# Ternary layers of a six-part transformer kernel: the first unit of each half multiplies part by part, and VectorE casts the second feature tile

## The reference

```
x = x + attention(layernorm(x))          # 16 heads
x = x + ternary_ffn(layernorm(x))        # called f0 here
x = x + gated_delta(layernorm(x))
x = x + ternary_ffn(layernorm(x))        # f1, same weights
x = x + attention(layernorm(x))          # 16 heads
x = x + routed_ffn(layernorm(x))
x = x + latent_attention(layernorm(x))
x = x + routed_ffn(layernorm(x))
```

```
scale = mean(|W|) + 1e-8
Wq    = clip(round(W / scale), -1, 1) * scale      # for W_up, W_gate (1024x256), W_down (256x1024)
up    = x @ Wq_up.T                                # 1024 x 1024
gate  = x @ Wq_gate.T
out   = (silu(up) * gate) @ Wq_down.T              # 1024 x 256
```

## Time and profile before

| what | us |
|---|---|
| median of three runs | 1550.88 |
| the three runs | 1550.71, 1550.88, 1554.65 |
| profiled execution, device time | 1545.75 |
| its span, first to last instruction | 1544.0 |
| TensorE matmuls busy | 1339.6 (87%) |
| VectorE busy | 919.0 (60%) |
| ScalarE busy | 681.9 (44%) |
| GpSimd busy | 305.8 (20%) |
| mean granted TensorE clock | 0.913 of full speed |

### The profile page before, as it was taken

The page is one execution under the profiler, slowest core; times in us unless marked ns, Lnnn a source line. Parts: engine busy times, 40 slices in busy tenths (PEclk is TensorE's granted clock), DMA queues, the critical chain, the costliest instruction groups (busy, mean ns, idle before and its releaser), DMA issues. The chain is left out here.

```text
span 1544.0 us, 31244 instructions
## 1 busy us (share of the span) xinstructions
PE 1339.6 (87%) x12873; PEld 752.5 (49%) x12881; DVE 919.0 (60%) x2164; ACT 681.9 (44%) x987; POOL 305.8 (20%) x394
## 2 busy tenths in 40 slices
PE   7999997987150998899999989999789999989999
PEld 3355544553130877363555545436235555555436
DVE  3899965744886246665999935433445555535431
ACT  5578786634250223644777762111334444442110
POOL 4340440001308000006100000110333434210110
PEclk9999998998665599998999998999679999998999
DMA  3222200000312100003222030000300000000000
GB/s 89 59 42 62 61 2 32 1 12 0 103 41 51 28 5 1 14 1 64 38 37 40 13 100 0 1 9 0 62 10 16 14 16 14 9 1 1 0 0 28
DMA packets 51808, 41.64 MB, mean 27 GB/s; under 512 B 26498, under 2 KB 41971, under 8 KB 51667
## 3 DMA queue, kind: packets, MB, share of 16 engines
q1 hardware_dynamic: 51666, 39.65, 11.9%
HBM read 20.33 MB, written 3.43 MB: 15 GB/s over the span
## 5 line engine op out<-in xcount | busy, mean ns | idle before, releaser
L586 DVE TENSOR_REDUCE row_max_pieces<-psum 128x1 f32<-128x512 f32 (+3 forms) x672 | 407.2, 647 | 125.0 <-PE psum L481 122.6
L685 ACT ACTIVATE probs<-psum 128x1024 f32<-128x1024 f32 (+7 forms) x384 | 343.8, 900 | 219.8 <-PE psum L481 219.4
L535 PE MATMUL psum<-probs,v_ones 128*32 128x256 f32 (+1 forms) x2688 | 239.3, 377 | 8.6 <-POOL probs L470 4.2
L481 PE MATMUL psum<-q_all,k_head 97*32 97x512 f32 (+3 forms) x1536 | 193.8, 497 | 3.5 <-issue 3.5
L481 PE MATMUL psum<-k_stack,q_stack 96*32 96x512 bf16 x2048 | 162.6, 387 | 5.5 <-DVE row_max_pieces L586 3.3
L481 PE MATMUL psum<-q_stack,k_stack 97*32 97x512 bf16 x2048 | 160.8, 385 | 0.0
L535 PEld LDWEIGHTS psum<-probs,v_ones 128*32 128x32 f32 x2688 | 88.6, 109 | 85.1 <-POOL probs L470 21.2
L481 PE MATMUL psum<-k_head_bf,q_all_bf 80*32 80x512 bf16 (+3 forms) x768 | 96.6, 349 | 5.2 <-POOL q_all_bf L2314 3.7
L481 PEld LDWEIGHTS psum<-q_all,k_head 97*32 97x32 f32 x1536 | 79.2, 110 | 34.9 <-issue 9.3
L481 PEld LDWEIGHTS psum<-k_stack,q_stack 96*32 96x32 bf16 x2048 | 58.2, 97 | 71.9 <-DVE row_max_pieces L586 20.4
L481 PEld LDWEIGHTS psum<-q_stack,k_stack 97*32 97x32 bf16 x2048 | 59.5, 97 | 50.7 <-issue 3.8
(11 more groups left out here) (324 smaller groups left out, 2096.0 us busy)
## 6 DMA issues: line engine op xcount, KB each, us to landing
q_stack<-arena SPq DMA_DIRECT2D x32, 96.0 KB, 2.7
k_stack<-arena SPq DMA_DIRECT2D x32, 96.0 KB, 2.7
arena<-gd_g_sums SPq DMA_DIRECT2D x6, 512.0 KB, 5.9
q_stack<-arena SPq DMA_DIRECT2D x32, 64.0 KB, 2.3
k_stack<-arena SPq DMA_DIRECT2D x32, 64.0 KB, 2.3
x_tokens<-in_x SPq DMA_DIRECT2D x4, 256.0 KB, 4.2
k_stack<-arena SPq DMA_DIRECT2D x32, 32.0 KB, 2.3
q_stack<-arena SPq DMA_DIRECT2D x32, 32.0 KB, 2.0
```

What stands on the lines that cost most here:

```text
L481: last = pe.matmul(o[j:j + 32], by[:, j:j + 32], rows, **flags)
L535: last = pe.matmul(psum[32 * g:32 * g + VW, PVB, a - g * D:D], V[:, c, h, :], pr[:, n % PB, a:(g + 1) * D], start=(c == 0), stop=(c == (2 ...
L586: last = dve.reduce_max(mx[:, h % 2, qt, i:i + 1], o[:, 0:plain], AX.X)
L685: act.activation(pr[:, n % PB, q_from(c):], psum[:, 2 * (n % 2):2 * (n % 2) + 2, :].rearrange("p a n -> p (a n)")[:, q_from(c):], ACT.Exp, ...
```

## The change

The semaphore `x_high_last` is new. In every half, ScalarE casts only k = 0 of the high part; VectorE casts k = 1 with a `tensor_copy` ahead of its first subtraction. TensorE no longer waits ahead of the first unit of a half for all low parts. In this unit it waits for the two high casts and multiplies the high part with up and with gate, then waits for the middle parts and does the same, then for the low parts. The other seven units of a half keep the order of before. Number and shape of the matmuls are unchanged, and so are the semaphores that they raise.

```diff
+    x_high_last = sem("_x_high_of_last_features")
...
-                    if e == 0:
-                        pe.wait_ge(x_low, KT * (half + 1))
                     if u >= 2:
                         pe.wait_ge(hid, u - 1)
-                    for j, w in enumerate((ups, gates)):
-                        for part in range(3):
-                            for k in range(KT):
-                                last = pe.matmul(psum[:, 2 * b + j, :], w[:, k, e * P:(e + 1) * P],
-                                                 XP[:, part, k, cols(half)],
-                                                 start=(part == 0 and k == 0), stop=(part == 2 and k == KT - 1))
-                        last.then_inc(proj, 1)
+
+                    def product(j, part):
+                        w = (ups, gates)[j]
+                        for k in range(KT):
+                            last = pe.matmul(psum[:, 2 * b + j, :], w[:, k, e * P:(e + 1) * P],
+                                             XP[:, part, k, cols(half)],
+                                             start=(part == 0 and k == 0), stop=(part == 2 and k == KT - 1))
+                        if part == 2:
+                            last.then_inc(proj, 1)
+
+                    if e == 0:
+                        pe.wait_ge(x_high, half + 1)
+                        pe.wait_ge(x_high_last, half + 1)
+                        for j in range(2):
+                            product(j, 0)
+                        pe.wait_ge(x_mid, KT * (half + 1))
+                        for j in range(2):
+                            product(j, 1)
+                        pe.wait_ge(x_low, KT * (half + 1))
+                        for j in range(2):
+                            product(j, 2)
+                    else:
+                        for j in range(2):
+                            for part in range(3):
+                                product(j, part)
...
-                    for k in range(KT):
-                        act.activation(XP[:, 0, k, cols(half)], XNT[:, k, cols(half)], ACT.Copy).then_inc(x_high, 1)
+                    act.activation(XP[:, 0, 0, cols(half)], XNT[:, 0, cols(half)], ACT.Copy).then_inc(x_high, 1)
...
+                    dve.tensor_copy(XP[:, 0, 1, cols(half)], XNT[:, 1, cols(half)]).then_inc(x_high_last, 1)
                     for k in range(KT):
-                        dve.wait_ge(x_high, half * KT + k + 1)
+                        dve.wait_ge((x_high, x_high_last)[k], half + 1)
                         dve.tensor_tensor(xr[:, k, cols(half)], XNT[:, k, cols(half)], XP[:, 0, k, cols(half)],
                                           ALU.subtract).then_inc(x_rest, 1)
```

## The result

Three comparisons of the two kernels were made, each on one chip. The first, with eight executions of each, is the result of record. In the third, one execution of the changed kernel was in a slow state (1572.63 us) and is left out.

What follows compares the result with a forecast made beforehand. TensorE, busy 87% of 1544.0 us, was taken as the bound. Gains of 1.59 and 2.10 us in the two ternary layers, 3.7 us together, taken from the median 1550.88 gave 1547.2 us; range 1542.8 to 1552.3.

Steps and rivals of the forecast that it cites:

- the two terms: Gains at unit 2 of the two ternary layers: 1.59 us in the first, 2.10 us in the second.
- the slow stretch at its longest: Outer case of slow-clock matmuls in both ternary layers: gains 1.59 and 1.37 us, 3.0 us in all.
- Step 2: Unit 0, between high, middle and low parts: the two new waits cost nothing at the slow clock.
- Step 3: End of units 0 and 1: 7 slow matmuls in the first ternary layer, unit 1 done at 261.46; 9 in the second.
- the sum's own outer case: First ternary layer, unit 0 with all 12 matmuls slow: units 0 and 1 done at 262.51.
- Step 4: Unit 2 waits for VectorE's first product: at 262.52 against 264.11 in the first ternary layer, 630.12 against 632.22 in the second.
- the chances 0.18, 0.13 and 0.03: Chances of a faster result: 0.18 from the forecast's own scatter, 0.13 for Rival A, 0.03 for B.
- the sum's passage to the end: Behind the ternary layers: their gains pass on to the next layers and the end, 3.7 us off the median.
- Rival A: Layers behind the first ternary one: the clock rises earlier there, 1 to 2 us more gain, about 1545.7 us; chance 0.13.
- B: Both ternary layers: the whole 2.74 us come through in each, 5.5 us, 1545.4 us; chance 0.03.
- C: Stall before unit 2 lowers the clock: 2.5 us lost per slow unit, 1552.3 us with one per layer; chance 0.06.
- D: End of the ternary layer: something there hides the gain, 1550.9 us; chance 0.08.

Runs made afterwards that it cites:

- cast_half0: Changed kernel, but VectorE casts k = 1 only in half 0 and ScalarE casts both tiles in half 1; ratio 0.9972 [0.9956, 0.9988] to the kernel before.
- after_delay_f0: Changed kernel with three idle ScalarE copies at the end of the first ternary layer; ratio 0.9967 [0.9951, 0.9983] to the kernel before.
- delay3_f1: Kernel before, with three idle ScalarE copies behind the last step of the second ternary layer; ratio 0.9995 [0.9980, 1.0010].
- delay6_f1: Kernel before, with six idle ScalarE copies behind the last step of the second ternary layer; ratio 1.0027 [1.0012, 1.0042].
- f0_only: Kernel before, with both parts of the change in the first ternary layer alone; ratio 0.9993 [0.9982, 1.0005].

## Why the prediction was wrong

**What held.** That VectorE's cast takes about 0.40 us and costs half 0 nothing: 0.43, and nothing. That TensorE starts 2.7 us sooner: 0.69 instead of 3.40 behind the first cast. That the SiLU slips by 0.32: 0.34. That the first product is late next in f1 and takes back part of the gain: it was, unit 2 at 630.19 against a forecast of 630.12, and cast_half0, which moves that product by 0.33 us, moved unit 2 by 0.33. The sizes of the two terms: 1.59 and 2.10 forecast, 1.6 and 2.0 in the first trace. In the other two traces of the changed kernel f1 gave 1.4, near the 1.37 that the sum had for the slow stretch at its longest.

**What failed inside the layers, without moving the sum.** Step 2 had TensorE run on into the middle parts, with k0's part needed first and k1's second. The code waits for both at once, and the trace has TensorE waiting to 256.77. Step 3 took seven slow matmuls over from before; the rise to full clock came at the same time as before, so the earlier start made them twelve, the sum's own outer case (262.51 without the stall). Step 4 had f0 bound by the product at 262.52. All twelve matmuls of unit 0 ran slow there, and with the stall in front of the middle parts TensorE itself came to 262.83; the product was at hand at 262.52. The 0.33 us at the end of f0 made up for it: the forecast's 1.59 was met by luck, with 1.23 from the steps that it named. A slip besides: the chances 0.18, 0.13 and 0.03 for a faster result add up to 0.34, not 0.32.

**The step that failed: the sum's passage to the end**, "The shift of 1.59 passes to the down products, the norm and the next layer" and "I apply the gain to the median". The sum counted the ternary layers alone and took every other layer at its old length. In the traces they did not keep it: the delta layer took 1.5 us back, the second attention layer added 2.0, and latent and last layer 1.8 in the mean: -1.6 + 1.5 - 2.0 - 2.0 - 1.8 = -5.9 us, with f1's term at its largest; with 1.4 for f1 it is -5.3, and the first routed layer adds -0.6. The three comparisons gave 3.9, 6.8 and 8.8, about 6.

How well is each term shown? The delta term is shown by one trace that only shifts the work (after_delay_f0), with its granted clock of 0.65 against 0.50, and by the group means, though three traces of 297 to 300 stand across both groups. Half of the attention term is shown: the sixteen matmuls differ by 1.0 us and follow the granted clock in the pair delay3_f1 and delay6_f1; the layer's whole 2.0 rests on group means that don't overlap. But these two terms nearly cancel (-0.5). What the measured gain has over the forecast, 2.3 us of about 6 and 5.1 of the 8.8 of record, must come mostly from the last terms and from the draw of executions, and for these there is no proof: the latent term rests on which of two kinds of latent layer a trace happened to show, and both kernels have both. So the step that failed is known, and where the surplus came from is open.

Rival A named the mechanism, in the delta layer and with 1 to 2 us more gain. There the sign was the other one (delta lost), and the rival had 0.13.

**The base.** 1550.88 was the median of three executions, and in the comparison of record it was right (1550.53): there the whole miss is in the gain. Later medians of the old kernel were 1546.6, 1549.1, 1548.1 and 1546.8, each of 31 or 35 executions, while the eight of the comparison of record gave 1550.5. The 8.8 us of that comparison are more than the traces can account for, and its interval and that of the second comparison don't meet (it ends at 0.9959, the other begins at 0.9961). Whether that is the chip or the draw of sixteen executions is open. With the medians of the second and third comparison, 1543.89 and 1542.9, the forecast's range would have held, which says how near the call was, not that it was right: a range of 9.5 us was drawn around a single sum while the old kernel's own executions spread over 8 to 10 us in every comparison (1543.66 to 1553.89 in the last).

**The other rivals.** B (all of 2.74 us in both layers) was rightly small: the SiLU stood where it had to. C (a stall that brings the grant down) didn't come: unit 2 of f1 behind the stall ran at the fast clock. D was half true of f0, by another way: f0_only's gain could not be measured, and the delta layer is where the traces have it given back. Rival A took the 7 and 9 slow matmuls of step 3 as a case of variation from run to run; they are two layers of one execution, and show no such variation by themselves. The drain that the Trainium skill adds to a table load (ScalarE: Activation LUTs, "What ACT_TABLE_LOAD costs") is not seen after the change either: load at 259.66, SiLU at 260.96.

## What to carry to other kernels

When a step is made shorter, look at what the next consumer waits for last: of 2.7 us that TensorE starts sooner in f1, 2.0 were left in one trace and 1.4 in two. In the first of these the first product stood behind a table load and half 1's preparation, and one cast moved off that ladder gave 0.33 us back. An earlier start in a slow stretch also buys slow matmuls: the rise to full clock stayed where it was. A gain of a few microseconds early in a kernel whose clock changes often need not be passed on as it is: the layers behind it start at another moment of the granted clock. So give the sum an uncertainty of some microseconds to both sides, and try a pure delay in the same place before crediting the edit. Where executions spread by 10 us, take the base from dozens of them and compare one trace with one trace only by layers.

## What the runs showed of the hardware

- The same program had spans of 1544.0, 1544.4 and 1555.1 us. Most of the difference was in the delta and latent layers (3.1 to 3.4 and 5.2 to 6.6 us), with a mean granted clock of 0.70, 0.73 and 0.65 in the first 75 us of the latent layer.
- The granted clock fell and rose at the same times of two traces though the work had moved: 0.50 from 253.6 to 260.2 us and 1.00 from 260.4 with TensorE starting at 257.5 or 254.8, and 0.50 from 325.3 to 326.0 with the last transposes at 325.04 or 323.77.
- A delay of 1.4 us behind f1 cost nothing that could be measured (0.9995 [0.9980, 1.0010]), one of 3.1 us cost 4.2 (1.0027 [1.0012, 1.0042]).
- The same sixteen f32 matmuls of 128x512 took 8.80, 9.21 or 9.8 to 9.9 us at mean granted clocks of 0.81, 0.77 and 0.71 to 0.72, by how much of the stretch at 1.2 GHz they met: 7.1 us and half of their time at that level in each of five traces. The Trainium skill (TensorE: Matmul & The Clock Gate, "What's actually happening") says that the number of slow matmuls varies from run to run; here it was also a systematic effect of where the kernel puts them, since the attention layers behind the old and the new f1 didn't overlap (230.4 to 231.5 and 228.1 to 229.4 us).
- A cast of 128x512 from f32 to bf16 on VectorE, SBUF to SBUF, took 0.42 to 0.43 us where a subtraction of that size took 0.69.
